# Graph network kernel, first layer: the subtraction of the running maxima moved from VectorE to two float32 matmuls in PSUM, products in halves of 1024 columns

## What is computed

```python
w_m = (efeat @ W_msg + b_msg).reshape(E, in_f, -1)
w_a = (efeat @ W_attn + b_attn).reshape(E, in_f, -1)
h_src = feat[src][:, :, None]
e1 = w_m * h_src
e2 = w_a * h_src
seg_max = jax.ops.segment_max(e2, dst, num_segments=N)
ex = jnp.exp(e2 - seg_max[dst])
denom = jax.ops.segment_sum(ex, dst, num_segments=N)
attn = ex / denom[dst]
ft = jax.ops.segment_sum(e1 * attn, dst, num_segments=N)
return ft.sum(axis=1)
```

## Time and profile before

| | us |
|---|---|
| median of three runs | 14537.35 |
| lowest, highest | 14511.41, 14591.29 |
| the profiled execution, its own time | 14542.93 |
| its span, first to last instruction | 14541.7 |
| DVE busy | 11137.2 (77%) |
| POOL busy | 8838.1 (61%) |
| PE busy | 8238.6 (57%) |
| ACT busy | 4787.7 (33%) |

### The profile page before, as it was taken

The page is one execution under the profiler, slowest core; times in us unless marked ns, Lnnn a source line. Parts: engine busy times, 40 slices in busy tenths (PEclk is TensorE's granted clock), DMA queues, the critical chain, the costliest instruction groups (busy, mean ns, idle before and its releaser), DMA issues. The chain is left out here.

```text
span 14541.7 us, 147837 instructions
## 1 busy us (share of the span) xinstructions
PE 8238.6 (57%) x41291; PEld 5764.4 (40%) x41291; DVE 11137.2 (77%) x19230; ACT 4787.7 (33%) x2765; POOL 8838.1 (61%) x6976
## 2 busy tenths in 40 slices
PE   1222222222220489689746565665678858985886
PEld 0111111111110367567523233332456646664664
DVE  6999999999998768578645455554578868886886
ACT  0110110110110368467501110110057746774774
POOL 5555555555553377678745555555168857885886
PEclk5555555555555799899867787777789979997997
DMA  2444444444442222222211111111033323332332
GB/s 81 157 150 155 157 152 153 157 154 151 157 155 94 68 68 84 60 71 82 55 45 37 38 36 37 36 35 38 16 102 111 112 74 105 112 106 80 111 110 70
DMA packets 629773, 1371.10 MB, mean 94 GB/s; under 512 B 262833, under 2 KB 403118, under 8 KB 554126
## 3 DMA queue, kind: packets, MB, share of 16 engines
q1 hardware_dynamic: 405534, 1076.25, 20.2%
q0 software_dynamic: 224112, 293.30, 8.8%
HBM read 656.16 MB, written 712.80 MB: 94 GB/s over the span
## 5 line engine op out<-in xcount | busy, mean ns | idle before, releaser
L536 POOL DMA_INDIRECT h<-in_x,idx x1568 | 2252.1, 1436 | 2000.3 <-DMA efT<-in_edge_attr_t 1561.3
L550 PE MATMUL PS<-waug,efT 17*128 17x256 f32 x6272 | 1129.7, 679 | 3165.9 <-DVE e L587 2178.7
L1684 PE MATMUL PS<-hot,lhs 128*128 128x392 bf16 x9408 | 1829.2, 352 | 1221.8 <-issue 644.4
L1671 POOL DMA_INDIRECT myg<-node_table,mix x1568 | 1644.5, 1049 | 1310.0 <-DVE mmsg L1740 782.1
L550 PEld LDWEIGHTS PS<-waug,efT 17*128 17x128 f32 x6272 | 696.7, 314 | 3598.4 <-DVE e L587 2225.4
L1684 PEld LDWEIGHTS PS<-hot,lhs 128*128 128x128 bf16 x9408 | 949.9, 102 | 2101.4 <-issue 1028.9
L1305 PE MATMUL PS<-every_weight,dstf 112*128 112x144 f32 (+1 forms) x8960 | 1346.4, 296 | 533.2 <-DVE dstf L1405 376.1
L1305 PEld LDWEIGHTS PS<-every_weight,dstf 112*128 112x128 f32 x8960 | 1268.1, 200 | 717.6 <-DVE dstf L1405 197.1
L1755 DVE TENSOR_TENSOR lhs<-mkx,m 128x512 bf16<-128x512 bf16 x1176 | 428.9, 419 | 1402.8 <-remote 1065.4
L571 ACT ACTIVATE cf<-cf 128x256 f32<-128x256 f32 x196 | 81.7, 417 | 3842.8 <-DVE e L614 3842.8
L1283 POOL DMA_INDIRECT c0yg<-node_table,c0ix x672 | 935.8, 1393 | 533.1 <-DMA c0ix<-in_src 287.4
(11 more groups left out here) (393 smaller groups left out, 18688.7 us busy)
## 6 DMA issues: line engine op xcount, KB each, us to landing
softmax_maxima<-M SPq DMA_DIRECT2D x196, 1024.0 KB, 8.2
softmax_denominators<-ST SPq DMA_DIRECT2D x196, 1024.0 KB
softmax_numerators<-ST SPq DMA_DIRECT2D x196, 1024.0 KB
r0rb<-pick_b SPq DMA_DIRECT2D x56, 512.0 KB
r0ra<-pick_a SPq DMA_DIRECT2D x56, 512.0 KB
r1rb<-pick_b SPq DMA_DIRECT2D x56, 512.0 KB
r1ra<-pick_a SPq DMA_DIRECT2D x56, 512.0 KB
c0rb<-pick_b SPq DMA_DIRECT2D x56, 512.0 KB
```

What stands on the lines that cost most here:

```text
L536: PO.indirect_dma_start(h[b.k][:, q, :], None, io["x"], bass.IndirectOffsetOnAxis(ap=idx[b.k][:, q:q + 1], axis=0))\
L550: mm = PE.matmul(PS[0:CH, 4 * message + 2 * (n % 2) + r, 0:C2], efT[b.k][row:row + D + 1, n // 2, :], waug[row:row + D + 1, C2 * message:C ...
L1671: PO.indirect_dma_start(yg[b.k][:, q, :], None, table8, bass.IndirectOffsetOnAxis(ap=ix[b.k][:, q:q + 1], axis=0))\
L1684: mm = PE.matmul(PS[:, 6 + k, 0:A7 // 2], lhs[(G * b.k + q) % 2][:, r, part, :], hot[4 * ((G * b.k + q) % 2) + r][:, k * A7 // 2:(k + 1) * ...
```

## The change

In place of DVE's subtraction the logits are put back into PSUM by PE: an identity matmul writes `e2` into a bank (`put_back`), and a second matmul with the negated identity (`minus`) adds `-M` onto it (`less_maxima`, now a function of `l0_tensor`). Each is float32, 128 x 128 by 512 columns, four of each per block, one pair per bank. ACT takes its exponentials from PSUM, in two halves of 1024 columns.

For that the attention weights occupy all of banks 0 to 3 (`wa`), two edge columns per bank, the message weights banks 4 to 7 (`wm`). Column q of a block is at place `at(q) = 2 * (q % 4) + q // 4` in `wa`, `wm`, `h`, `e2` and the `P` of `PX`, so that a bank gets only matmuls of one group of 32 rows. Half 0 holds columns 0, 1, 4 and 5, half 1 the columns 2, 3, 6 and 7. `weigh`, `logits` and `messages` work in halves: four matmuls, and 1024 columns of DVE, per call. The attention weights of a half may be written once ACT has read that half of the block before (`l_ex`). Half 1 comes first, as its banks 2 and 3 need the maxima of columns 2, 3, 6 and 7 only.

```diff
+        minus = sb("minus_ident", [128, 128], F32, L)
+        wa = PS[0:CH, 0:4, :].rearrange("p b (t c) -> p (b t) c", c=C2)
+        wm = PS[0:CH, 4:8, :].rearrange("p b (t c) -> p (b t) c", c=C2)
...
+        def at(q):
+            return 2 * (q % 4) + q // 4
...
-            def weigh(b, n, message):
-                if not message:
+            def weigh(b, half, message):
+                if message:
+                    if due(m := b.on(-1).count(2, half + 1)):
+                        PE.wait_ge(l_p, m)
+                else:
                     PE.wait_ge(l_in[b.k], b.slot(32, 32))
-                if due(m := b.count(4, n - 1)):
-                    PE.wait_ge(l_p if message else l_e2, m)
-                for r in TWO:
-                    row = 32 * (2 * (n % 2) + r)
-                    mm = PE.matmul(PS[0:CH, 4 * message + 2 * (n % 2) + r, 0:C2], efT[b.k][row:row + D + 1, n // 2, :],
+                    if due(m := b.on(-1).count(3, 2 - half)):
+                        PE.wait_ge(l_ex, m)
+                for q in (2 * half, 2 * half + 1, 2 * half + 4, 2 * half + 5):
+                    row = 32 * (q % 4)
+                    mm = PE.matmul((wm if message else wa)[:, at(q), :], efT[b.k][row:row + D + 1, q // 4, :],
                                    waug[row:row + D + 1, C2 * message:C2 * message + C2])
                 mm.then_inc(l_wm if message else l_wa, 1)
+            def put_back(b, n):
+                PE.wait_ge(l_e2, b.count(2, 2 - n // 2))
+                PE.matmul(PS[0:CH, n, :], ident[:, :], e2[b.k % 2][:, 2 * n:2 * n + 2, :], start=True, stop=False)
+
+            def less_maxima(b, n):
+                PE.wait_ge(l_bw, b.count(TB0 - 1, TB0 - 1 - n))
+                mm = PE.matmul(PS[0:CH, n, :], minus[:, :], M[b.k][:, n::4, :], start=False, stop=True)
+                if n % 2 == 0:
+                    mm.then_inc(l_le, 1)
+
             def body(b):
-                for n in range(4):
-                    weigh(b, n, 0)
+                for half in (1, 0):
+                    weigh(b, half, 0)
                 if b.on(-1).exists():
-                    for n in range(4):
-                        weigh(b.on(-1), n, 1)
+                    for half in TWO:
+                        weigh(b.on(-1), half, 1)
+                for n in (3, 2, 1, 0):
+                    put_back(b, n)
+                for n in (3, 2, 1, 0):
+                    less_maxima(b, n)
...
-                S.activation(P[:, 0, :, :], e[:, :, :], ACT.Exp).then_inc(l_ex, 1)
+                S.activation(PX[b.k % 2][:, 0, 4 * half:4 * half + 4, :], wa[:, 4 * half:4 * half + 4, :], ACT.Exp).then_inc(l_ex, 1)
...
-            def less_maxima(b):
-                e = e2[b.k % 2]
-                V.wait_ge(l_bw, b.count(TB0 - 1, TB0 - 1))
-                V.tensor_tensor(e[:, :, :], e[:, :, :], M[b.k][:, :, :], ALU.subtract).then_inc(l_a, 1)
...
             def body(b):
                 last = b.on(-1) if b.on(-1).exists() else None
+                logits(b, 1)
                 logits(b, 0)
...
```

More of the change, by code:

```diff
@@ L471, in l0_first_vector @@
             V.wait_ge(*l_clear.now())
+            V.wait_ge(*vd.now())
         def l0_first_sync():
@@ L561, in last, with exp_half @@
             def last(b):
-                for n in range(4):
-                    weigh(b, n, 1)
+                for half in TWO:
+                    weigh(b, half, 1)
             loop(PE, body, NB0, TB0, last=last, u=U0)
         def l0_scalar():
[L568 to L571, removed]
+            def exp_half(b, half):
+                S.wait_ge(l_le, b.count(2, 2 - half))
@@ L572, in body @@
                 if due(n := b.on(-2).count(TB0, TB0)):
                     S.wait_ge(l_s, n)
-                S.activation(P[:, 0, :, :], e[:, :, :], ACT.Exp).then_inc(l_ex, 1)
+                S.activation(PX[b.k % 2][:, 0, 4 * half:4 * half + 4, :], wa[:, 4 * half:4 * half + 4, :], ACT.Exp).then_inc(l_ex, 1)
+            def body(b):
+                exp_half(b, 1)
+                exp_half(b, 0)
+                S.wait_ge(l_a, b.count(1, 1))
+                S.activation(cf[b.k % 2][:, :], cf[b.k % 2][:, :], ACT.Exp).then_inc(l_ex, 1)
@@ L576, in l0_scalar, with logits @@
             loop(S, body, NB0, TB0, u=U0)
         def l0_vector():
-            def logits(b, n):
-                ts = slice(2 * n, 2 * n + 2)
-                if n == 0:
+            def logits(b, half):
+                ts = slice(4 * half, 4 * half + 4)
+                if half == 1:
                     V.wait_ge(l_g[b.k], b.slot(16 * TB0, 16 * TB0))
[L583 to L586, removed]
+                V.wait_ge(l_wa, b.count(2, 2 - half))
@@ L635, in carried @@
                     V.wait_ge(l_st[b.k], n)
+                V.wait_ge(l_ex, b.count(3, 3))
                 if due(n := b.count(TB0, 0)):
@@ L639, in carried, with messages @@
                                 bc(cf[b.k % 2][:, :], 2, 1), ALU.mult).then_inc(l_q, 1)
-            def messages(b, n):
-                ts = slice(2 * n, 2 * n + 2)
+            def messages(b, half):
+                ts = slice(4 * half, 4 * half + 4)
                 P = PX[b.k % 2]
                 V.wait_ge(l_t, b.count(1, 1))
-                V.wait_ge(l_wm, b.count(4, n + 1))
-                bank = 4 + 2 * (n % 2)
-                V.tensor_tensor(P[:, 1, ts, :], PS[0:CH, bank:bank + 2, 0:C2], P[:, 1, ts, :], ALU.mult).then_inc(l_p, 1)
+                V.wait_ge(l_wm, b.count(2, half + 1))
+                V.tensor_tensor(P[:, 1, ts, :], wm[:, ts, :], P[:, 1, ts, :], ALU.mult).then_inc(l_p, 1)
             def sum_step(b, q):
                 s, P = ST[b.k], PX[b.k % 2]
-                V.wait_ge(l_p, b.count(4, q // 2 + 1))
+                V.wait_ge(l_p, b.count(2, 1 if q < 2 else 2))
                 if q == 0:
                     V.wait_ge(l_q, b.count(1, 1))
-                    V.tensor_tensor(s[:, :, 0, :], s[:, :, 0, :], P[:, :, 0, :], ALU.add).then_inc(l_s, 1)
+                    V.tensor_tensor(s[:, :, 0, :], s[:, :, 0, :], P[:, :, at(0), :], ALU.add).then_inc(l_s, 1)
                 else:
@@ L669, in body @@
                 last = b.on(-1) if b.on(-1).exists() else None
+                logits(b, 1)
                 logits(b, 0)
[L671 removed]
                 forward(b, 0)
[L673 removed]
+                if last:
+                    exp_by_source(last)
                 forward(b, 1)
[L675 removed]
+                if last:
+                    carried(last)
                 forward(b, 2)
                 if last:
[L678 removed]
+                    messages(last, 0)
                 forward(b, 3)
[L680 to L681 removed]
                 forward(b, 4)
                 if last:
[L684 removed]
+                    sum_step(last, 0)
                 forward(b, 5)
+                forward(b, 6)
+                if last:
+                    sum_step(last, 1)
+                forward(b, 7)
                 if last:
                     messages(last, 1)
[L688 to L694 removed]
+                for n in range(7):
+                    backward(b, n)
                 if last:
                     sum_step(last, 2)
[L697 to L714 removed]
+                    sum_step(last, 3)
                 factor(b)
[L716 to L718 removed]
+                for q in range(4, TB0):
+                    if last:
+                        sum_step(last, q)
             loop(V, body, NB0, TB0, last=sums_alone, u=U0)
```

42 lines of the change are left out of this document (10 added, 32 removed).

## The result

| | us |
|---|---|
| kernel before, median of 4 runs | 14534.86 (14511.41 to 14591.29) |
| changed kernel, median of 4 runs | 14829.94 (14805.23 to 14839.87) |
| ratio, 95% interval | 1.0195 (1.0162 to 1.0227) |
| forecast, its range | 14576 (14455 to 14710) |

A forecast was written before the change was run, and what follows sets the result against it. DVE's time per block was taken as the bound: 21.39 us plus a 0.6 wait for PE made 21.99, 0.20 more than before; over 196 blocks +39 us, so 14576 us, range 14455 to 14710.

The forecast's parts named there:

- What DVE gains (2.87 a block) and gives back (2.47): DVE per block: subtraction, larger logits pieces and a dropped wait save 2.87 us; 13 dependent neighbour pairs cost 2.47.
- The price of a maxima pair: DVE's backward steps in a row: each needing its neighbour costs 0.19 us more, starts 0.583 apart.
- Rival 4: DVE's neighbouring steps cost nothing, as the skill says; PE's chain binds near 20 us a block, 14190 us; chance 0.03.
- The wait for PE (0.6, of 0 to 1.0): DVE's second logits piece waits 0.6 us a block for PE's chain, which starts at half clock.
- the forecast's 21.99: Forecast time per block of the stage: 21.39 us of DVE plus a 0.6 wait, 0.20 more than before.
- rival 1: DVE's wait for PE vanishes, by early clock rise or no fall; 21.39 us a block, 14459 us; chance 0.20.
- The sum for DVE: DVE's own time per block after the change, gains and neighbour costs counted: 21.39 us, 0.40 less than before.
- The stage's start and end change by under 3 us: Outside the 196 equal blocks, the changed stage's beginning and end add or remove less than 3 us.
- Rival 3: PE stays at half clock throughout the stage, DVE waits 2.5 us a block; 14950 us; chance 0.10.

The follow-up runs named there:

- e9_balanced: Changed kernel with 32 memsets ahead of the loop, DVE's order rewritten to move independent work and leave more behind the fourth backward step; 0.9822 of the kernel before.
- e1_pad32: Changed kernel with 32 small DVE memsets ahead of the first layer's loop, moving only its place in the code; 0.9947 of the kernel before.
- e3_pad256: Changed kernel with 256 small DVE memsets ahead of the loop, the same place relative to a 256-instruction line; 1.0206 of the kernel before.
- e12_pad12: Changed kernel with 12 small DVE memsets ahead of the first layer's loop; 0.9941 of the kernel before.
- e4_late_stores: Changed kernel with SP holding back a block's stores until DVE's first logits product two blocks on; 1.0090 of the kernel before.
- e5_before_pad235: Kernel before the change with 235 small DVE memsets ahead of its loop; 1.0081 of the kernel before without them.
- e2_before_pad225: Kernel before the change with 225 small DVE memsets ahead of its loop; 1.0010 of the kernel before without them.
- e11_two_copies: Changed kernel with 32 memsets, DVE reordered with less work behind the backward steps, and PE copying each logits bank twice; 1.0071 of the kernel before.
- e6_spread: Changed kernel with 32 memsets, PE's three later logits copies held until DVE made 2, 5 and 8 forward steps; 0.9981 of the kernel before.

## Why the prediction was wrong

**What DVE gains (2.87 a block) and gives back (2.47).** Right in kind, but the second is too large by some 0.4. The seven backward steps stand in a row and take 3.59 us, 0.52 apart against the 0.583 of the earlier trace rows: six of the pairs cost 0.12 each, not 0.19. The four sum steps (3.31 us) start 0.85 apart, 0.19 over their slot, as the earlier trace rows said. The price of a maxima pair was taken from the first block, and why the same pair costs 0.19 there and 0.12 in the loop was not tried. Rival 4 falls: neighbours do cost, and an order with fewer of them (`e9_balanced`: 9 in place of 13) and enough work behind the chain's start is what gained. The sentence of the Trainium skill beside it (VectorE: DVE Perf Modes, "The DRAIN you can't avoid") doesn't hold for such steps: 0.395 us from start to start without the dependence, 0.52 with it.

**The wait for PE (0.6, of 0 to 1.0).** It is 62.7 us over the stage in `e1_pad32`, 0.32 a block. The clock did what the rows said: down in the pause, up while the subtraction runs (in the changed kernel 0.50, 0.58 and 1.00 in the windows of 2 us from 4206 to 4212). Together the stage has 4159.2 / 195 = 21.33 us a block where it had 21.76, 0.66 under the forecast's 21.99. That it meets rival 1's 21.39 is in part luck: rival 1 has no wait, while here DVE alone takes 21.01 and waits 0.32. The sum for DVE was 0.38 too high and the wait 0.28, and both erred to the same side. A kernel with only these terms is 0.9947 of the one before, or about 14458 us on the first chip, at the lower end of my range.

**The step that failed** is the sentence "The stage's start and end change by under 3 us" and what it takes for granted, that a block costs the same wherever the loop stands in the code and wherever in its turn the block is. I summed one block and multiplied by 196. The term that was left out is 371 us, 47 waits in 49 turns. With 20 us more of waiting for PE (83.0 against 62.7) and one wait of 21.5 us elsewhere it is the whole 411 us between the changed kernel and `e1_pad32` (4570.0 less 4159.2). On one chip, `e3_pad256` against `e1_pad32`, it is 360. None of the rivals had it. Rival 3, half clock throughout, came nearer in time, with a mechanism that isn't there. The loop's length and by how much it moved could be counted ahead of the run from the built code, and would have shown the risk. Where the border lies could not: only `e1_pad32`, `e3_pad256` and `e12_pad12` place it. Nor could the price per turn: a row under "issue" with a fetch beside it doesn't exist in the trace of before.

## What to carry to other kernels

Count a hot loop's instructions per engine, and where it begins. Lines of 256, two of them held, fit all the runs here; by them a loop of 258 to 512 instructions reaches over a third line or not depending on its place (268 instructions in 11 places of 256, 303 in 46), and any edit ahead of it can change that. Look in the profile for the instruction queue's packets and for idle time under "issue" once per turn, and move the loop by a few instructions before judging the edit. Stores issued at the turn's end make such a fetch dearer: 8.1 us against 4.5. And an interleaving by hand should leave behind the step that releases another engine just as much work as that engine's chain takes: here 7 us, where 4.4 lost all that the better order gained.

## What was unexpected of the hardware

- A fetch at the loop's turn stops DVE for 4.5 us with DMA idle and 8.1 us behind three stores of 1 MB (418 GB/s); the old loop, at such a place, loses 2.5 us or next to nothing. About 230 more packets cost 360 us of the stage (`e3_pad256`), 203 (`e4_late_stores`), 109 (`e5_before_pad235`) or 8 (`e2_before_pad225`).
- PE's granted clock fell in a pause of 6.3 us behind 16 us of matmuls nearly without a gap (`e11_two_copies`), and within a pause of 2.6 us in one block of `e6_spread`, though in the blocks on either side the copy behind a pause as long still took 1.13 and 1.25 us; in that block, three copies of 2.0 to 2.1 us with pauses of 0.6 and 1.0 us between them all ran at 0.50.
- A step that reads its neighbour's result starts 0.12 us late at 256 columns in the loop, 0.19 at 512; between the last logits (1024 columns) and the first forward step DVE shows 0.21 us of idle time.
